# Moving three experts of each pair into the next pair, and convolving two channel pairs on TensorE with folded weights

## The chip, the cores and the metric

The kernel runs on one core of one Trainium2 chip, in one launch. The metric is the device time of that launch in microseconds (us). A core has TensorE (matmuls, with the loading of their weights as instructions of their own), VectorE, ScalarE, GpSimd and SyncE, which here issues most of the DMAs; they run their own instruction lists and meet through semaphores. TensorE's clock is granted at one of two levels, 1.2 or 2.4 GHz, and the profile shows which (0.50 or 1.00).

## The reference, cut to what matters

Eight sequences of 256 tokens with 128 channels pass two layers, all in float32:

```python
x = x + gated_delta(layernorm(x))        # layer 0: 8 key heads, 16 value heads of 64
x = x + moe_176(layernorm(x))            # layer 0: 8 routed experts (best 2), 1 shared, hidden 176
x = x + attention_block(layernorm(x))    # layer 1: 16 heads of 8, then a dense MLP 128-512-128
x = x + moe_512(layernorm(x))            # layer 1: 1 shared and 8 routed experts (best 2), hidden 512

# inside gated_delta
mixed = hidden @ W_qkv.T                                       # 2048 channels
y = conv(mixed over time, conv_w, 4 taps, causal, depthwise)   # one filter per channel
mixed = silu(y)                                                # then queries, keys, values

# moe_512
shared_out + sum_e gates[..., e] * (gelu(x @ up[e]) @ down[e]) + x
```

The convolution is linear and has one filter per channel, so that `y[t] = sum_k conv_w[:, k] * (W hidden[t - 3 + k])`: the tap can be multiplied into the weights first.

## The kernel before, in words

**Phase 1** (lines 727 to 815 on ScalarE, 1197 to 1294 on TensorE, 1751 to 1816 on VectorE) is the gated delta layer. It is written out for ten turns; in a turn three sequences are at work: `i` has its outputs and its state computed, `n` its decays, its key products and the inverse of its triangular blocks, `f` its projections and its convolution. Sixteen tiles of 128 channels are projected in eight pairs (`project`, L979, one PSUM bank per pair): pairs 0 and 1 are queries, 2 and 3 keys, 4 to 7 values. For each pair ScalarE copies the last tap's product out of PSUM (`seed`, L602), VectorE adds the three other taps with six multiply-adds (`convolve`, L1595) and ScalarE applies silu (`silu`, L611). TensorE multiplies keys with queries and keys (`key_products`, L1012), VectorE scales the products by the decays (L1663, L1665) and inverts the 32x32 blocks in 62 small steps (L1677, L1680), between which it does the elementwise work of sequence `i`; its last step (L1687) releases TensorE's small solves (`solve32`, L1050 and L1051), which are followed by merges (L1062 to L1076). Before them TensorE makes the output gates (`gate`, L961). The products of the queries with the state (`from_state`, L1160) are taken by VectorE at L1747.

**Phase 2** (`pair_layers` on each engine) takes two sequences, 512 tokens, at a time. Its four steps on TensorE are: the first experts' up matmuls (L1330) and down matmuls (L1348 to L1360), whose results VectorE merges in chunks of 128 tokens (L1900, semaphore `merged`) and normalises twice (`norm`, L1559 to L1572); the attention, from the transposes of the normalised tokens (L1308) over the projections (L1365), the rotated queries and keys (VectorE L1923 to L1927, TensorE L1374), scores (L1394, L1400), softmax and values to the output projection (L1489); after a layernorm the dense MLP (L1494, gelu L895, L1499); after another the router (L1314) and the nine experts (`up`, L1513, gelu on ScalarE L903, `down`, L1522, and VectorE's accumulation into `x2`, L1977). The order on TensorE is up(0), and then up(e + 1) and down(e) for each expert. Behind down(4) the tokens of the next pair are transposed (`turn_first`). Pairs 0 to 2 run in a hardware loop (`Fori`), pair 3 is written out behind it. SyncE loads the next pair once all four chunks are merged and stores a pair when its last expert has been added.

The order of all this is written by hand: each engine's list is fixed, and the semaphore counts in the waits say what must have ended.

## Time and profile before

| | us |
|---|---|
| median of 3 runs (lowest, highest) | 1685.59 (1682.43, 1690.14) |
| the profiled execution | 1669.67 |
| its span, first to last instruction | 1667.9 |
| TensorE busy in the span | 1368.3 (82%) |
| VectorE busy | 911.9 (55%) |
| ScalarE busy | 723.2 (43%) |
| GpSimd busy | 195.3 (12%) |
| mean granted TensorE clock | 0.843 |

The times are of one execution taken by the hardware profiler, from the start of the span. Phase 1 ends near 816 us with the first load of phase 2. A busy share says little by itself here: both phases are chains in which the bound moves from one engine to another. PE is TensorE's matmuls, PEld its weight loads, DVE VectorE, ACT ScalarE, POOL GpSimd, SP SyncE. A float32 matmul stands in the profile as two instructions, each with its own weight load, so that four matmuls of 512 columns are counted as x8.

### The profile page before, as it was taken

How to read it: one execution, taken by the hardware profiler on the slowest of the kernel's cores; microseconds unless marked ns; L12 is line 12 of the kernel's file. 1: busy time of each engine (PE TensorE's matmuls, PEld its weight loads, DVE VectorE, ACT ScalarE, POOL GpSimd, SP SyncE). 2: the span in 40 equal slices, each digit the busy share in tenths (PEclk: the TensorE clock that was granted, in tenths of full speed). 3: DMA queues.
4: the chain of work that ended last, by engine and by line, in shares of the span. 5: the costliest groups of instructions: out<-in, count | busy, mean ns of one | idle time of the engine just before them, and what ended most of it. 6: DMA issues, size and time to landing. Idle time of an engine off the chain costs nothing.

```text
span 1667.9 us, 27801 instructions
## 1 busy us (share of the span) xinstructions
PE 1368.3 (82%) x11040; PEld 984.9 (59%) x11048; DVE 911.9 (55%) x2365; ACT 723.2 (43%) x1347; POOL 195.3 (12%) x188
## 2 busy tenths in 40 slices
PE   2768897988879888878588789877899768997689
PEld 2456666676757667568455466653676435764356
DVE  4687979787887969681354222552224621255221
ACT  1646473746565564724232333423324233342332
POOL 5011212112121212110100000000000000000000
PEclk9768898887978787876796899968999689996899
DMA  3000000000000000003000000000000000000000
GB/s 113 4 1 4 2 11 1 1 10 2 10 2 10 2 7 2 29 1 138 12 7 1 1 1 8 1 7 1 1 8 1 7 1 1 7 1 1 1 0 7
DMA packets 15076, 17.80 MB, mean 11 GB/s; under 512 B 2567, under 2 KB 13216, under 8 KB 14560
## 3 DMA queue, kind: packets, MB, share of 16 engines
q1 hardware_dynamic: 12768, 14.09, 2.6%
q8 instruction: 91, 1.49, 0.4%
q0 software_dynamic: 576, 1.76, 0.3%
q10 hardware_dynamic: 1600, 0.12, 0.1%
q14 instruction: 41, 0.34, 0.1%
HBM read 13.87 MB, written 2.10 MB: 10 GB/s over the span
## 4 chain that ended last, share of the span: by engine, by line
PE 36%; issue 32%; DVE 23%; ACT 6%; POOL 2%; DMA 1%; SPq 0%; POOLq 0%; DVEq 0%; ACTq 0%
PE ps L1012 4%; DVE arena L1677 4%; DVE arena L1680 4%; PE ps L1513 4%; PE ps L1522 4%; PE ps L994 4%; DVE arena L1595 2%; PE ps L1494 1%; PE ps L1330 1%; PE ps L979 1%; POOL rstd L508 1%; PE ps L1138 1%; ACT arena L611 1%; PE ps L991 1%; PE ps L1125 1%
## 5 line engine op out<-in xcount | busy, mean ns | idle before, releaser
L1595 DVE SCALAR_TENSOR_TENSOR arena<-ps,conv_w,arena 128x255 f32<-128x255 f32 (+2 forms) x384 | 163.6, 475 | 19.5 <-ACT arena L602 15.0
L1522 PEld LDWEIGHTS ps<-arena 128*128 128x128 f32 x1152 | 133.7, 192 | 15.3 <-issue 14.6
L903 ACT ACTIVATE arena<-ps 128x512 f32<-128x512 f32 x144 | 86.0, 597 | 127.9 <-PE ps L1513 127.9
L1513 PE MATMUL ps<-arena 128*128 128x512 f32 x288 | 135.3, 617 | 0.0
L1522 PE MATMUL ps<-arena 128*128 128x128 f32 x1152 | 133.8, 275 | 0.0
L1977 DVE SCALAR_TENSOR_TENSOR arena<-ps,rw,arena 128x128 f32<-128x128 f32 x128 | 36.0, 343 | 139.0 <-PE ps L1522 139.0
L508 POOL TENSOR_TENSOR rstd<-var_eps,half_power 128x2 f32<-128x2 f32 (+1 forms) x28 | 23.3, 832 | 748.2 <-DVE var_eps L1566 748.2
L1012 PE MATMUL ps<-arena 64*128 64x256 f32 x256 | 84.0, 468 | 16.4 <-ACT arena L611 16.4
L1012 PEld LDWEIGHTS ps<-arena 64*128 64x128 f32 x256 | 53.4, 225 | 62.3 <-DVE arena L1665 27.2
L1663 DVE TENSOR_TENSOR arena<-ps,arena 128x512 f32<-128x512 f32 x64 | 44.1, 689 | 84.2 <-PE ps L1012 73.9
L468 POOL TENSOR_TENSOR arena<-con,log_decay 128x512 f32<-128x512 f32 x64 | 68.3, 1078 | 178.4 <-PE ps L994 78.5
L1513 PEld LDWEIGHTS ps<-arena 128*128 128x128 f32 x288 | 55.0, 200 | 57.1 <-issue 57.1
L979 PE MATMUL ps<-arena 128*128 128x256 f32 x256 | 80.7, 450 | 8.8 <-DVE arena L1595 8.0
L1680 DVE TENSOR_TENSOR arena<-arena 128x30 f32<-128x30 f32 (+14 forms) x240 | 83.1, 346 | 8.2
L1677 DVE TENSOR_TENSOR arena<-arena 128x30 f32<-128x30 f32 (+14 forms) x240 | 83.0, 346 | 7.0
L994 PE MATMUL ps<-arena,con 128*128 128x512 f32 x128 | 83.8, 743 | 0.0
L581 ACT ACTIVATE arena<-ps,log_beta 128x128 f32<-128x128 f32 x256 | 70.9, 378 | 29.0 <-PE ps L994 28.7
L1308 PE MATMUL ps<-con,h_tok 128*128 128x128 f32 x48 | 13.4, 435 | 82.0 <-DVE h_tok L1572 82.0
L979 PEld LDWEIGHTS ps<-arena 128*128 128x128 f32 x256 | 53.6, 226 | 31.1 <-DVE arena L1595 17.9
L482 POOL TENSOR_TENSOR o_rstd<-ssq,half_power 128x16 f32<-128x16 f32 x16 | 47.0, 2936 | 212.6 <-DVE ssq L1715 212.6
L602 ACT ACTIVATE arena<-ps,conv_w 128x256 f32<-128x256 f32 x128 | 51.7, 485 | 44.9 <-PE ps L979 44.6
L1935 DVE TENSOR_REDUCE arena<-ps 128x8 f32<-128x2048 f32 (+1 forms) x24 | 54.3, 2289 | 30.6 <-PE ps L1400 30.6
(247 smaller groups left out, 2988.5 us busy)
## 6 DMA issues: line engine op xcount, KB each, us to landing
arena<-in_routed_up SPq DMA_DIRECT2D x1, 2048.0 KB, 9.9
arena<-in_routed_down SPq DMA_DIRECT2D x1, 2048.0 KB, 14.5
x_ln<-in_x SPq DMA_DIRECT2D x8, 128.0 KB, 2.3
arena<-in_w_mix SPq DMA_DIRECT2D x1, 1024.0 KB, 9.7
x_in<-in_x SPq DMA_DIRECT2D x8, 128.0 KB, 2.5
...
```

The lines of the kernel that those rows point to most:

```text
L468: pool.tensor_tensor(gm[k % NB].rearrange("p (h n) -> p h n", h=BATCH), over_heads(upto, BATCH), over_last(log_decay[n % 2][:, c, BATCH * ...
L581: ins = act.activation(dm[n % 2][:, BATCH * k + h, :], ps[:, k % 2, h * P:(h + 1) * P], ACT.Exp, bias=log_beta[n % 2][:, c, v:v + 1])
L903: act.activation(hid1[e % 2][:, i, :], ps[:, i, :], ACT.Gelu).then_inc(s["mgelu"], 1)
L979: mm = pe.matmul(ps[:, PAIR_BANK[p], j * SEQ:(j + 1) * SEQ], w_mix[:, m * P:(m + 1) * P], hT3[:, f % 3, :], start=True, stop=True)
L994: pe.matmul(ps[:, k % 2, :], beyond, gm[k % NB], start=False, stop=True, skip_group_check=True)\
L1012: mm = pe.matmul(ps[:, KK_BANK[k % 2], 2 * P * g:2 * P * (g + 1)].rearrange("p (q n) -> p q n", q=2), mix_qk[n % 2][r:r + DH, QK_TILES + m ...
L1513: pe.matmul(ps[:, i, :], m_up[:, e, i * P:(i + 1) * P], hT, start=True, stop=True)\
L1522: mm = pe.matmul(ps[:, 4 + e % 2, c * P:(c + 1) * P], hid1[e % 2][:, i, c * P:(c + 1) * P], m_down[:, e, i, :], start=(i == 0), stop=(i == ...
L1595: ins = dve.scalar_tensor_tensor(conv_tile(f, m)[:, sh:SEQ], ps[:, PAIR_BANK[p], j * SEQ:(j + 1) * SEQ - sh], conv_w[:, m, TAPS - 1 - sh:T ...
L1677: me.did(dve.tensor_tensor(tmp, inv[:, j + 1:BLOCK, j:j + 1].to_broadcast([P, rows, j]), inv[:, j:j + 1, 0:j].to_broadcast([P, rows, j]), ...
L1680: me.did(dve.tensor_tensor(inv[:, j + 1:BLOCK, 0:j], inv[:, j + 1:BLOCK, 0:j], tmp, ALU.subtract))
L1935: dve.tensor_reduce(heads, sc, X_AXIS, ALU.max, negate=True).then_inc(s["max_ready"], 1)
```

## The change

Experts: the last three of the nine (6, 7 and 8) of pairs 0 to 2 are no longer computed at the end of their pair but at three places of the next pair; pair 3 keeps all nine. Their input `hT_m` (the transposed tokens) and the sum `x_m` get storage of their own, the gates too, and a pair is stored when its ninth accumulation has been made. All loops over pairs are written out. The attention's weights are loaded after phase 1 instead of in its last turns, because `eps` now lies in the storage of `xs64`.

Convolution: for channel pairs 0 and 1 four weight matrices each with one tap multiplied in (`w_tap`) are made once at the start, by sixteen scaled identities on VectorE, four matmuls with ones that spread a tap over the partitions, and four products. TensorE then makes projection and convolution of such a tile in four matmuls over shifted columns that accumulate in PSUM, and ScalarE applies silu straight from PSUM. The two pairs drop out of `seed`, `convolve` and `silu`, and pair 2 is projected where pair 0 was.

VectorE makes the folded weights once, at the start:

```diff
+            dve.memset(v_tok[:, 0, 0:2, :], 1.0).then_inc(s["tap_ones"], 1)
+            for m in range(2 * FOLDED):
+                for tap in range(TAPS):
+                    dve.tensor_scalar(w_tap[:, m, tap, :], ident, conv_w[:, m, tap:tap + 1], None, ALU.mult)\
+                        .then_inc(s["tap_diag"], 1)
+            for m in range(2 * FOLDED):
+                dve.wait_ge(s["tap_psum"], m + 1)
+                dve.tensor_tensor(w_tap[:, m, :, :], ps[:, m, :].rearrange("p (a b) -> p a b", a=TAPS),
+                                  over_heads(w_mix[:, m * P:(m + 1) * P], TAPS), ALU.mult).then_inc(s["taps_ready"], 1)
```

TensorE in phase 1:

```diff
+            def convolve_folded(f, m, n, has_n):
+                p, j = m // 2, m % 2
...
+                for sh in range(TAPS):
+                    mm = pe.matmul(ps[:, PAIR_BANK[p], j * SEQ + sh:(j + 1) * SEQ], w_tap[:, m, TAPS - 1 - sh, :],
+                                   hT3[:, f % 3, 0:SEQ - sh], start=(sh == 0), stop=(sh == TAPS - 1), skip_group_check=True)
...
-                    project(f, 0, n, has_n)
+                    project(f, 2, n, has_n)
...
-                    project(f, 1, n, has_n)
+                    convolve_folded(f, 0, n, has_n)
                 if has_i:
                     from_state(i, 0, (6, 7), (("s_ready", i + 1), ("r_ready", 2 * i + 1)), "qs_psum")
                     solve(i, 1, 0)
                 if has_f:
-                    project(f, 2, n, has_n)
+                    convolve_folded(f, 1, n, has_n)
...
                             gate(i, n, c, j, has_i)
+                if has_f:
+                    convolve_folded(f, 2, n, has_n)
+                    convolve_folded(f, 3, n, has_n)
+                if has_n:
                     solve32(i, n, 0, has_i)
```

ScalarE in phase 1 (the second call stands ahead of `solved32`; the seeds and silus of pairs 0 and 1 go):

```diff
-                    seed(f, 0)
-                    seed(f, 1)
+                    silu_folded(f, 0)
...
+                if has_f:
+                    silu_folded(f, 1)
```

SyncE in phase 2:

```diff
+            for it in range(PAIRS):
+                if it + 1 < PAIRS:
+                    sp.wait_ge(s["merged"], G * it + G)
+                    sp.dma_start(pair_in[:, :, :], pair(out, it + 1)).then_inc(s["pair_loaded"], 16)
+                if it > 0:
+                    sp.wait_ge(s["mdown_used"], EXPERTS * it)
+                    sp.dma_start(pair(out, it - 1), x_m[:, :, :]).then_inc(s["x_stored"], 16)
```

TensorE in phase 2, behind the first FFN's down matmuls, behind the output projection and behind the dense MLP's down matmuls:

```diff
+                if it > 0:
+                    pe.wait_ge(s["merged"], it * G + 2)
+                    up(it - 1, LATE[0], LATE_BANKS[0])
+                    pe.wait_ge(s["merged"], it * G + G)
+                    down(it - 1, LATE[0], LATE_DOWN[0], 0)
                 turn_tokens(1, h_tok, 4)
...
+                if it > 0:
+                    up(it - 1, LATE[1], LATE_BANKS[1])
+                    down(it - 1, LATE[1], LATE_DOWN[1], 1)
                 turn_tokens(2, h_tok, 5)
...
+                if it > 0:
+                    up(it - 1, LATE[2], UP_BANKS)
+                    down(it - 1, LATE[2], LATE_DOWN[2], 1)
+                turn_tokens(3, h_tok, 6)
+                route(hT_m, m_rt[:, :])
+                up(it, 0, UP_BANKS)
+                here = LATE[0] if more else EXPERTS
+                for e in range(here):
+                    if e + 1 < here:
+                        up(it, e + 1, UP_BANKS)
+                    down(it, e, 4 + e % 2, e % 2)
                     if more and e == AHEAD:
                         turn_first(it + 1)
```

ScalarE in phase 2, the first late expert's gelus between two table switches (the others stand ahead of `transpose_out(2)` and `transpose_out(3)`):

```diff
+                if it > 0:
+                    load_table(ACT.Gelu)
+                    hidden(it - 1, LATE[0], LATE_BANKS[0], 0)
                 load_table(ACT.Exp)
```

VectorE in phase 2, ahead of the rotation (the two others stand behind `norm(5)` and `norm(6)`), and the loops of all engines:

```diff
+                if it > 0:
+                    accumulate(it - 1, LATE[0], LATE_DOWN[0])
...
-            with pe.Fori(0, PAIRS - 1) as it:
-                pair_layers(it, True)
-            pair_layers(PAIRS - 1, False)
+            for it in range(PAIRS):
+                pair_layers(it, it + 1 < PAIRS)
```

`LATE` is (6, 7, 8), `LATE_BANKS` ((0, 1, 0, 1), (1, 2, 3, 5)), `LATE_DOWN` (6, 6, 5). `up` waits for the gelus of the expert before only where the banks are still in use; `down` waits for its gelus and for the accumulation two experts back.

## Rows read from the trace of the kernel before

**Rows 1.** Stretches: from:to, length, busy us (PE, PEld, DVE, ACT, POOL), clock, DMA share, GB/s

```profile
1080.30:1089.60 9.30, 0.00 (x0) 0.00 (x0) 7.45 (x34) 0.00 (x0) 1.39 (x2) 0.67 0.10 29
1152.00:1158.50 6.50, 0.00 (x0) 0.00 (x0) 5.23 (x15) 0.27 (x2) 3.50 (x3) 0.74 0.00 0
...
1186.00:1241.00 55.00, 55.00 (x323) 40.54 (x322) 9.79 (x39) 20.44 (x34) 1.02 (x1) 1.00 0.00 1
```

**Rows 2.** Chain that ended last, router and first experts of pair 2: start us, us, what

```profile
1389.24 1.87 PE ps L1314 x8
1391.11 8.51 PE ps L1513 x16
1399.62 3.57 PE ps L1522 x32
1403.19 3.44 PE ps L1513 x8
```

**Rows 3.** The same chain, the dense MLP's first matmuls of pairs 1, 2 and 3

```profile
1160.53 6.12 PE ps L1494 x8
...
1372.16 6.11 PE ps L1494 x8
...
1580.53 6.04 PE ps L1494 x8
```

**Rows 4.** TensorE in order of time, pair 1: start, us, what, [idle before <- releaser]

```profile
1089.65 1.12 PE L1308 MATMUL ps<-con,h_tok 128*128 128x128 f32 x4 [9.36 <-DVE h_tok L1572]
1091.64 5.49 PE L1365 MATMUL ps<-arena 128*128 128x384 f32 x8 [0.87 <-ACT arena L830]
...
1101.37 0.81 PE L1394 MATMUL ps<-causal_bf,ident_bf 128*128 128x512 bf16 x3
```

**Rows 5.** TensorE in order of time, end of the attention to the router, pair 1

```profile
1150.82 1.16 PE L1489 MATMUL ps<-arena 128*128 128x128 f32 x8 [0.69 <-ACT arena L890]
1158.54 1.11 PE L1308 MATMUL ps<-con,h_tok 128*128 128x128 f32 x4 [6.56 <-DVE h_tok L1572]
...
1175.81 1.12 PE L1308 MATMUL ps<-con,h_tok 128*128 128x128 f32 x4 [4.57 <-DVE h_tok L1572]
```

**Rows 6.** VectorE in order of time, second merge's layernorm and last rotation, pair 1

```profile
1084.79 0.49 DVE L1559 BATCH_NORM_STATS2 stats<-arena 128x6 f32<-128x128 f32 x2
...
1098.64 0.42 DVE L1927 TENSOR_TENSOR arena<-arena 128x256 f32<-128x256 f32 x1
```

**Rows 7.** ScalarE in order of time, ahead of the key products, one sequence

```profile
485.62 0.84 ACT L602 ACTIVATE arena<-ps,conv_w 128x256 f32<-128x256 f32 x2 [2.51 <-PE ps L979]
...
494.92 0.63 ACT L611 ACTIVATE arena<-arena 128x512 f32<-128x512 f32 x1
```

**Rows 8.** TensorE's waits in one turn of the pair loop: us in total, times, longest

```profile
PE ps L1314 <- issue: 2.1, 1, 2.1
```

**Rows 9.** VectorE in order of time, the last two convolutions of that sequence

```profile
490.60 5.28 DVE L1595 SCALAR_TENSOR_TENSOR arena<-ps,conv_w,arena 128x255 f32<-128x255 f32 x12 [1.42 <-ACT arena L602]
```

**Rows 10.** TensorE in order of time, projection and query-times-state products, next sequence

```profile
537.37 1.03 PE L979 MATMUL ps<-arena 128*128 128x256 f32 x4
538.33 1.16 PE L1160 MATMUL ps<-arena 64*128 64x128 f32 x16
```

**Rows 11.** TensorE, the first of the small solves in two sequences

```profile
378.92 0.21 PE L1050 MATMUL ps<-arena 32*32 32x32 f32 x1 [1.43 <-DVE arena L1687]
...
562.70 0.26 PE L1050 MATMUL ps<-arena 32*32 32x32 f32 x1 [4.75 <-DVE arena L1687]
```

**Rows 12.** A stretch of the sequence of the 1.43 us row (columns as in rows 1)

```profile
353.00:366.00 13.00, 13.00 (x55) 12.29 (x54) 11.61 (x25) 4.35 (x10) 2.98 (x1) 0.50 0.01 1
```

**Rows 13.** VectorE, GpSimd and TensorE at the start, each in order of time

```profile
21.07 0.60 DVE L1572 TENSOR_SCALAR h_tok<-x_ln,mv,rstd 128x128 f32<-128x128 f32 x2 [2.40 <-POOL rstd L454]
...
17.49 2.85 POOL L447 TENSOR_SCALAR arena<-arena,norm_w 128x1024 f32<-128x1024 f32 x1 [3.00 <-DMA arena<-in_w_out]
...
20.48 1.94 PE L923 MATMUL ps<-con 128*128 128x128 f32 x8 [20.48 <-POOL arena L447]
```

254 lines of the change are left out of this document (141 added, 113 removed).

## The prediction

> **What bounds the kernel now.** I read the stretches table first, then each stretch's own chain of waits, then each engine in order of time around the places that the diff touches. Phase 1 (the gated delta layer, eight sequences in one unrolled pipeline) ends near 816 us and phase 2 (four pairs) takes the rest. The pairs repeat: the first 512-column matmuls of the dense MLP start at 1160.53, 1372.16 and 1580.53 us [rows 3], so a pair takes 211.63 us inside the loop and 208.37 us where pair 3, written out behind the loop, follows pair 2.
>
> Inside a pair the reader is to see two kinds of stretch. The expert stretch is pure TensorE: busy 55.00 of 55.00 us at full clock, VectorE 9.79, ScalarE 20.44 [rows 1]. Its chain is a strict alternation of 3.44 us (four up matmuls) and 3.57 us (four chunks of down) [rows 2], 7.01 us per expert. The other kind is TensorE standing still for a layernorm: 9.36 us ahead of the attention [rows 4], 6.56 and 4.57 us ahead of the dense MLP and the router [rows 5], at a granted clock of 0.67 and 0.74 of 2.4 GHz on the mean of the first two [rows 1]. What follows them runs at the lower level, 1.2 GHz: eight 512-column instructions took 6.12 us [rows 3], where the same shape takes 3.44 us in the expert stretch [rows 2].
>
> Phase 1 is a ring of all engines. Per sequence (about 92.6 us) the ends that matter are: ScalarE's last silu ahead of the key products [rows 7]; VectorE, without a pause, from the products through the 32x32 inverse; and TensorE's small solves, which start when VectorE's inverse is turned [rows 11].
>
> **Phase 2, experts moved.** Experts 6, 7 and 8 of pairs 0 to 2 leave the expert stretch: 3 pairs x 3 x 7.01 = 63.1 us off the path. They come back, each as eight up and 32 down instructions, at three places of the next pair.
>
> (a) Behind the first FFN's down matmuls, ahead of the attention's transposes. The place is 9.36 us long [rows 4]. Up costs 3.44 us plus about 0.3 us for two waits on the gelus (only two banks), then the wait for the fourth merged chunk, which VectorE ends some 4.5 us into the gap (the second layernorm pair begins at 1084.79 [rows 6]), then down, 3.57: it ends about 1.2 us before the transposes can start. Cost 0. The cover is the two layernorms; without them it would be 7.9 us. What is queued behind that wait on TensorE is only the down itself. ScalarE pays two more table switches and four gelus while it has no other work. VectorE's four accumulations (1.13 us, the price of the other experts' groups) stand ahead of the rotation, where it waits for the projections anyway. Since TensorE no longer rests, I expect the transposes (1.12) and the projections (5.49 us, 1.37 a chunk [rows 4]) at half these times. The first chunk is then ready 0.5 + 0.7 = 1.2 us earlier, and VectorE's rotation, whose last operation ends at 1098.64 + 0.42 = 1099.06 now [rows 6], ends at 1097.9. TensorE, which now begins the query and key transposes only behind all projections and needs some 4.2 us for them, has one of four chunks left by then, 1.05 us. So the scores start 9.3 us behind the first transposes and not 11.7 (1089.65 to 1101.37 [rows 4]): 2.4 us gained.
>
> (b) Behind the output projection: 1150.82 + 1.16 = 1151.98 to 1158.54 is free [rows 5]. Up 3.44, last gelu 0.7, down 3.57: it ends at 1159.8, 1.3 us late. (c) Behind the dense MLP's down: 3.44 + 0.7 + 3.57 = 7.7 us in a gap of 4.57, so 3.1 us late. Against that, everything from 1158.5 on meets a warm array: the eight MLP instructions 3.44 instead of 6.12, two sets of transposes 0.65 instead of 1.12, the route about 1.1 instead of 1.87 and the first two ups 6.88 instead of 8.51 [rows 2, 3, 5]. From the end of the output projection to the end of the second up it takes 36.0 us now and 3.44 + 0.7 + 3.57 + 1.6 + 3.44 + 0.8 + 3.6 + 3.44 + 0.7 + 3.57 + 1.4 + 1.1 + 6.88 = 34.2 us then: 1.8 us gained with two experts inside.
>
> So pairs 1 to 3 gain 2.4 + 1.8 = 4.2 us each, 12.6 us. The store of a pair now waits for its ninth accumulation in the next pair, and VectorE's first accumulation there waits for that store: it has over 10 us (route, two ups, one down) for one transfer, cost 0; on SyncE the load of the next pair stands ahead of it and needs nothing of it. The attention weights are now fetched behind the first pair's load instead of before phase 2's start; they are wanted 60 us later, cost 0 to 1 us.
>
> (d) The loops over pairs are written out. At the loop's turn TensorE waits 2.1 us, once per turn, for nothing but issue [rows 8] and the clock falls; the turn without a loop is the 3.26 us shorter one. Two turns: 6.5 us. Phase 2 together: 63.1 + 12.6 + 6.5 = 82.2 us less.
>
> **Phase 1, two pairs of channels on TensorE.** Removed per sequence: 12 of VectorE's 48 multiply-adds (5.28 us for twelve [rows 9]), four ScalarE copies, two silus over SBUF, four 256-column matmuls. Added: sixteen 256-column matmuls and two silus from PSUM. The 5.3 us of VectorE buy nothing by themselves: the last two convolutions wait for ScalarE's copies, 1.42 us in the row [rows 9], and these wait for TensorE's projections; both stay where they are. What counts is ScalarE's queue, which is full from 485.6 until the last silu ends at 495.55 [rows 7]; two silus of about 0.55 us leave it: 1.1 us, seven times, 7.7 us gained. The last convolution then ends last, and caps it there.
>
> Costs. One matmul of 256 columns is 0.5 us (1.03 for two, tail included [rows 10]) at full clock and 0.86 at half. First, four matmuls stand in place of two ahead of the query-times-state products; those end at 538.33 + 1.16 = 539.49 [rows 10], just when VectorE asks for them (it had no pause there): no slack where the clock is low; I estimate 1 us where it is full, from the two groups ahead at half their time. So 0.9 us in two of six sequences, 1.8. Second, the last eight matmuls (3.5 us) go into TensorE's rest ahead of the small solves, 4.75 us in one sequence, 1.43 us in another, which follows 13 us at half clock [rows 11, 12]. With the 0.9 us pushed in front, cost 0 in four sequences and 1.5 and 5 in two: 6.5 us. If the cover were gone it would be 4.4 us each. Third, a busier TensorE keeps the clock a little longer into the solves; I take 0.5 us x 7 = 3.5 us gained. The bounds are 0 and the 4.7 us that the half-clock work there could give back.
>
> The Trainium skill speaks against the folding: its page "TensorE: Matmul & The Clock Gate", section "Part 3: Packing small matmuls", has weight loads overlap running matmuls only where row groups differ, and gives 128 / 1.2 ns for one. By that rule the 24 added instructions would each show 0.107 us, 2.6 us a sequence, and the sum would come out 21 us longer. The trace does not agree: 32 full-height down instructions of 128 columns, each with its own load, take 3.57 us, 0.112 each [rows 2], with no room for a load.
>
> **The start.** VectorE now makes sixteen scaled identities (128x128) and four folded weights (128x512, behind one matmul each) before the first layernorm, whose result was there at 21.67 us [rows 13]. The trace has no such scaling; the nearest are 0.30 us for one 128x128 normalisation, two in 0.60 [rows 13], so about 4.8 us from 17.7 on, and beside GpSimd's 2.85 us [rows 13] perhaps later. TensorE is held until 20.48 and has 1.94 us of transposes [rows 13]; then four 512-column matmuls (3.44 us at full clock [rows 2], twice that at half), and VectorE's last product 0.7: 29.3 us. The layernorm itself, with GpSimd's root in it, takes about 2.4 (the row before shows 2.40 of waiting for GpSimd, most of it for the 2.85 us operation). Its result comes at about 31.7, 10 us late; six convolutions instead of eight then make up 5.3 us. Cost 5 us, bounds 0 and 10.
>
> Phase 1 together: -7.7 + 1.8 + 6.5 - 3.5 + 5 = +2 us.
>
> **The sum.** 1669.7 us (the profiled execution; its span is 1667.9) - 82 + 2 = 1589.7, a ratio of 0.952. The median of the runs shown is 1685.59, 1% above the profiled one; the same ratio gives 1605 us.
>
> **The rivals.** (1) Phase 1 spills: TensorE's rest ahead of the solves is too short in most sequences. 5 us more in each of seven, 35 us: 1640 us. For it: the 1.43 us row [rows 11]; against: 4.75 us. (2) Weight loads show: each of the 24 instructions added per sequence waits for its own load, 40.54 / 322 = 0.126 us [rows 1], 3.0 us a sequence, 24 us in eight: 1629 us. Against it: the 0.112 us per down instruction [rows 2]. (3) The clock is kept through the dips of phase 1: what took half clock ahead of the key products and behind them halves, some 5 us in each of seven: 1570 us. (4) The gaps grant only half clock to the moved experts: 14.0 us each in places of 9.4, 6.5 and 4.6 us is 21.6 us late against 21.0 saved; phase 2 keeps only the loop's gain: 1680 us, no change. Against: the clock was 1.00 before each gap and the moved work leaves no rest. (5) Slower: all twelve additional matmuls of a sequence lie on the path at half clock, 12 x 0.86 = 10.3 us, eight times, plus 10 at the start, 92 us against 82: 1697 us. It decides once TensorE has no rest left ahead of the solves and of the state products, which needs half clock through the 92.6 us of a sequence; 4.75 us of rest [rows 11] says no.
>
> **Chances.** Forecast 0.68, (1) 0.12, (2) 0.03, (3) 0.11, (4) 0.03, (5) 0.03. The range reaches 27 us down, most of the way to (3), and to (1) above: 1578 to 1640. About 0.5% is what a measurement of this kernel can tell from no change; so faster 0.94, same 0.03, slower 0.03.
>
> **What would show it.** Starts of the dense MLP's matmuls 187 to 189 us apart from pair to pair, at 3.4 us for eight; six alternations in pairs 0 to 2 and nine in pair 3; waits of TensorE for the layernorm at the three places 1.3 us or none; a late expert in each at 3.44 and 3.57; the scores 9.3 us behind the transposes. In phase 1: the first layernorm's result near 31.7 us, ScalarE's queue 1.1 us shorter, small solves starting on VectorE's turn in most sequences. Wrong it would be if the clock's mean falls in phase 2, if VectorE or ScalarE ends last in the late experts, or if phase 1's length moves by more than 15 us.

## The result, and the profile after

The changed kernel takes 1604.11 us (median; 1602.58 to 1605.23) against 1684.01 us (1676.69 to 1690.14) of the kernel before, a ratio of 0.954 with a 95% interval of 0.952 to 0.957. The forecast was 1605 us. Run once more among the experiments, it came to 0.959 (0.956 to 0.962). The profiled execution took 1602.58 us with a span of 1600.7.

The traces of the two profiled executions differ by less than that: 1667.9 - 1600.7 = 67.2 us of span, where the medians differ by 79.9. The execution of before that was profiled was near the short end of its runs. Where the 67.2 us lie is read from the starts of the dense MLP. The chain that ended last in the changed kernel shows them (start us, us, what), with the late expert ahead of the one in pair 1:

```profile
958.90 5.71 PE ps L1582 x8
...
1137.34 3.45 PE ps L1425 x8
1141.46 3.84 PE ps L1434 x32
...
1146.61 3.71 PE ps L1582 x8
...
1330.98 3.71 PE ps L1582 x8
...
1515.31 3.71 PE ps L1582 x8
```

The pairs are 187.7, 184.4 and 184.3 us apart, where they were 211.6, 211.6 and 208.4 [rows 3 has the last three starts; the first was 948.9]. From the first of these starts to the last it is 556.4 us and was 631.6, 75.2 less; from the last to the end 85.4 and was 87.4. That is 77.2 us gained in phase 2. But the first start came at 958.9 and not at 948.9: ten microseconds lost ahead of it.

The expert stretch behind the first two ups is what it was [rows 2], 3.44 and 3.57 in turn, six times and not nine. What changed is what was the gaps [rows 1, 4, 5]. The stretches table (from:to, length, busy us of PE, PEld, DVE, ACT, POOL, clock, DMA share, GB/s):

```profile
1072.00:1090.00 18.00, 14.43 (x128) 10.56 (x128) 10.98 (x33) 6.33 (x14) 1.37 (x2) 0.98 0.06 16
...
1146.00:1161.00 15.00, 12.93 (x65) 8.40 (x66) 3.69 (x17) 5.69 (x9) 2.29 (x2) 1.00 0.00 0
```

The granted clock is 0.98 and 1.00 where the gaps of before had 0.67 and 0.74 [rows 1]. TensorE in order of time at the first place of pair 1 (start, us, what, [idle before <- releaser]):

```profile
1066.26 3.70 PE L1425 MATMUL ps<-arena 128*128 128x512 f32 x8
1070.94 3.84 PE L1434 MATMUL ps<-arena 128*128 128x128 f32 x32 [0.98 <-DVE arena L2003]
1075.78 0.66 PE L1362 MATMUL ps<-con,h_tok 128*128 128x128 f32 x4 [1.00 <-DVE h_tok L1655]
1077.37 2.85 PE L1447 MATMUL ps<-arena 128*128 128x384 f32 x8 [0.93 <-ACT arena L852]
...
1085.04 1.03 PE L1479 MATMUL ps<-causal_bf,ident_bf 128*128 128x512 bf16 x4
```

The late expert ends at 1074.78; the transposes still wait 1.00 us for VectorE's layernorm, where they waited 9.36 [rows 4]. They and the projections take half their time, and the first score instructions stand 9.26 us behind the transposes (11.72 before). The other two places:

```profile
1136.18 1.16 PE L1574 MATMUL ps<-arena 128*128 128x128 f32 x8 [0.69 <-ACT arena L923]
...
1145.14 0.60 PE L1362 MATMUL ps<-con,h_tok 128*128 128x128 f32 x4
1146.61 3.70 PE L1582 MATMUL ps<-arena 128*128 128x512 f32 x8 [0.87 <-ACT arena L852]
1151.09 3.84 PE L1587 MATMUL ps<-arena 128*128 128x128 f32 x32 [0.78 <-ACT arena L930]
...
1162.72 0.60 PE L1362 MATMUL ps<-con,h_tok 128*128 128x128 f32 x4
1164.01 1.06 PE L1368 MATMUL ps<-m_rt,arena 128*128 128x8 f32 x8 [0.69 <-ACT arena L850]
1164.92 7.11 PE L1425 MATMUL ps<-arena 128*128 128x512 f32 x16
```

No wait for a layernorm is left there: both late experts overrun their gaps. From the end of the output projection (1137.34) to the end of the second up (1172.04) it takes 34.70 us with two experts inside. Neither the store of a pair nor the later fetch of the attention's weights shows a wait: the only DMA wait of phase 2 on the compute engines is 4.8 us for the first pair's load, and it was 4.7 before.

Phase 1 has two places to look at. VectorE in order of time, where it multiplies the query-times-state products, then where it turns the inverse:

```profile
446.08 1.29 DVE L1830 TENSOR_TENSOR arena<-ps,ends 128x512 f32<-128x512 f32 x2 [0.99 <-PE ps L1210]
...
652.39 2.23 DVE L1770 STREAM_TRANSPOSE arena<-arena 128x1024 f32<-128x1024 f32 x1
```

and TensorE ahead of the small solves in two sequences:

```profile
377.70 2.09 PE L1028 MATMUL ps<-arena 128*128 128x253 f32 x9
380.37 0.21 PE L1100 MATMUL ps<-arena 32*32 32x32 f32 x1 [0.57 <-DVE arena L1770]
...
652.76 2.95 PE L1028 MATMUL ps<-arena 128*128 128x255 f32 x13
655.64 0.21 PE L1100 MATMUL ps<-arena 32*32 32x32 f32 x1
```

In the upper two rows the folded matmuls (L1028) end in time and TensorE waits for VectorE's turned inverse. In the lower two they run on until 655.7, past the end of the turning (654.62), and the solves start 3.25 us behind the start of the turning, not 2.23: the kind of spill that was forecast, here 1.0 us.

### The profile page after: what moved, and what is told of

Its sections match the earlier page's. It is cut to its first block, busy times and chain, and to the rows that moved or that the text cites. A ratio compares the mean times of both kernels' runs of the same rounds, so it can differ in the third digit from the quotient of the medians.

```text
span 1600.7 us, 27174 instructions
## 1 busy us (share of the span) xinstructions
PE 1389.8 (87%) x11248; PEld 1007.2 (63%) x11248; DVE 878.9 (55%) x2290; ACT 717.6 (45%) x1321; POOL 193.0 (12%) x186
## 4 chain that ended last, share of the span: by engine, by line
PE 65%; DVE 21%; ACT 8%; issue 3%; POOL 1%; DMA 1%; SPq 0%; ACTq 0%; DVEq 0%; POOLq 0%
PE ps L1434 7%; PE ps L1425 7%; PE ps L1384 6%; PE ps L1062 5%; PE ps L1044 4%; DVE arena L1760 3%; DVE arena L1763 3%; ACT arena L914 2%; PE ps L1485 2%; PE ps L1188 2%; DVE arena L2003 2%; PE ps L1517 2%; PE ps L1028 2%; PE ps L1120 2%; PE ps L1015 2%
## 5 line engine op out<-in xcount | busy, mean ns | idle before, releaser
L866 ACT ACTIVATE arena<-ps 128x512 f32<-128x512 f32 x144 | 85.3, 597 | 163.6 <-PE ps L1425 163.5
L1678 DVE SCALAR_TENSOR_TENSOR arena<-ps,conv_w,arena 128x253 f32<-128x253 f32 (+2 forms) x288 | 123.3, 475 | 53.3 <-ACT arena L613 49.9
L1434 PEld LDWEIGHTS ps<-arena 128*128 128x128 f32 x1152 | 133.2, 192 | 25.5 <-issue 11.0
L1924 DVE SCALAR_TENSOR_TENSOR arena<-ps,gates,arena 128x128 f32<-128x128 f32 x128 | 36.0, 344 | 131.4 <-PE ps L1434 131.4
L1425 PEld LDWEIGHTS ps<-arena 128*128 128x128 f32 x288 | 52.9, 194 | 56.2 <-issue 51.9
L592 ACT ACTIVATE arena<-ps,log_beta 128x128 f32<-128x128 f32 x256 | 70.9, 378 | 26.1 <-PE ps L1044 25.8
L914 ACT ACTIVATE arena<-ps 128x512 f32<-128x512 f32 x96 | 49.6, 602 | 46.1 <-PE ps L1517 46.1
L1188 PE MATMUL ps<-arena 128*128 128x64 f32 x512 | 69.8, 301 | 0.0
L1188 PEld LDWEIGHTS ps<-arena 128*128 128x128 f32 x512 | 69.3, 218 | 0.3
L1986 DVE SCALAR_TENSOR_TENSOR arena<-ps,b,arena 128x512 f32<-128x512 f32 x56 | 41.4, 749 | 48.6 <-ACT arena L877 48.3
## 6 DMA issues: line engine op xcount, KB each, us to landing
arena<-in_routed_down SPq DMA_DIRECT2D x1, 2048.0 KB, 12.9
arena<-in_w_mix SPq DMA_DIRECT2D x1, 1024.0 KB, 10.9
```

What stands on the lines that cost most here:

```text
L592: ins = act.activation(dm[n % 2][:, BATCH * k + h, :], ps[:, k % 2, h * P:(h + 1) * P], ACT.Exp, bias=log_beta[n % 2][:, c, v:v + 1])
L866: act.activation(hid1[half][:, i, :], ps[:, banks[i], :], ACT.Gelu).then_inc(s["mgelu"], 1)
L914: act.activation(probsT[u % 2][:, j, :], ps[:, 4 + j, :], ACT.Exp).then_inc(s["probs_ready"], 1)
L1188: mm = pe.matmul(ps[:, (7, 5)[g], h * DH:(h + 1) * DH], dm[i % 2][:, VH * c + v, :], eps[:, v, :], start=True, stop=True)
L1425: pe.matmul(ps[:, banks[i], :], m_up[:, e, i * P:(i + 1) * P], hT_m, start=True, stop=True)\
L1434: mm = pe.matmul(ps[:, bank, c * P:(c + 1) * P], hid1[half][:, i, c * P:(c + 1) * P], m_down[:, e, i, :], start=(i == 0), stop=(i == HT1 - 1))
```

## The experiments

Two ways of reading are used: the ratio to before, whose interval is about 0.004 wide on either side (6 us), and the parts of the profiled execution. This table is worked out from the order-of-time views of each; all times in us. "Inverse" is the start of the last turned inverse of phase 1, "stretch" goes from there to the first dense MLP, "pairs" are the distances of the dense MLPs, "tail" is the rest of the span, and "solves" is the length of the last sequence's second-chunk solves.

| kernel | ratio (95%) | inverse | stretch | pairs | tail | solves |
|---|---|---|---|---|---|---|
| before | 1 | 744.8 | 204.1 | 211.6 211.6 208.4 | 87.4 | 3.79 |
| whole change | 0.954 (0.952-0.957) | 744.7 | 214.2 | 187.7 184.4 184.3 | 85.4 | 6.53 |
| e1 late only | 0.953 (0.949-0.957) | 742.6 | 206.6 | 189.2 183.8 184.4 | 85.4 | 3.78 |
| e2 fold only | 1.001 (0.998-1.004) | 749.5 | 210.0 | 211.6 211.7 208.4 | 87.3 | 6.54 |
| e3 loops only | 0.995 (0.993-0.998) | 747.9 | 214.1 | 205.7 210.3 208.0 | 87.3 | 6.28 |
| e4 first place only | 0.983 (0.978-0.987) | 745.4 | 207.0 | 198.6 201.0 198.1 | 87.2 | 3.78 |
| e5 second, third place | 0.967 (0.963-0.970) | 743.6 | 206.3 | 198.7 194.6 194.6 | 85.3 | 3.78 |
| e6 filled gaps | 0.982 (0.978-0.986) | 746.2 | 207.5 | 207.3 201.3 201.4 | 84.0 | 3.79 |
| e7 query first | 0.955 (0.951-0.958) | 748.2 | 214.3 | 187.7 184.4 184.3 | 85.4 | 6.54 |
| e8 warm pair 0 | 0.947 (0.944-0.951) | 749.0 | 202.8 | 180.1 186.2 184.4 | 85.3 | 3.78 |
| e9 whole again | 0.959 (0.956-0.962) | 750.6 | 213.8 | 189.2 183.8 184.4 | 85.4 | 6.34 |
| e10 shifted | 0.954 (0.950-0.958) | 752.4 | 213.5 | 189.2 183.8 184.4 | 85.3 | 6.44 |
| e11 warm, fold | 0.947 (0.944-0.950) | 744.0 | 199.5 | 182.4 187.6 184.4 | 85.3 | 3.78 |
| e12 warm, no fold | 0.949 (0.946-0.952) | 742.3 | 209.5 | 180.1 186.2 184.4 | 85.3 | 6.76 |

**One part alone.** e1 has the changed phase 2 with phase 1 of before, here against the changed kernel:

```diff
-FOLDED = 2
-NC = NP - FOLDED
...
                 if has_f:
-                    convolve_folded(f, 0, n, has_n)
+                    project(f, 1, n, has_n)
```

> The kernel before with phase 2 alone changed: three late experts per pair, loops over pairs written out, phase 1 as before (all eight channel pairs convolved by VectorE). Theory, phase 2 carries the whole gain: the sum gave -82 us for phase 2 and +2 for phase 1, so this kernel should be 75 to 84 us faster than the kernel before, a ratio of 0.951 to 0.955, and no slower than the whole change. First dense MLP instructions of the pairs 184 to 188 us apart. Rival, the folding carries part: then it is 5 us or more slower than the whole change (1609 us and above). What is asked besides: in the changed kernel the stretch from the last inverse of phase 1 to the first dense MLP was 10 us longer, 5.7 of it small matmuls of the last sequence at half clock. If the folding does that, it is gone here, and this kernel is some 5 us faster than the whole change (about 1599 us).

Measured: 1600.43 us, ratio 0.9528. The whole gain is here, and nothing is missing without the folding. In the profiled execution, the fastest of its six, the stretch is 206.6 us and the last sequence's solves take 3.78 us; so most of the ten microseconds, 7.6, are not lost there. Whether for want of folding, the next runs say.

e2 is the other half, against the kernel before; phase 2 keeps its loops and nine experts in each pair:

```diff
+FOLDED = 2
+NC = NP - FOLDED
...
                 if has_f:
-                    project(f, 1, n, has_n)
+                    convolve_folded(f, 0, n, has_n)
```

> The kernel before with phase 1 alone changed: two channel pairs on TensorE with folded weights; phase 2 with its loops as before (the attention weights are fetched behind the first pair's load, since the small-solve buffers now cover their place). Theory: the terms of phase 1 as predicted sum to +2 us (-7.7 ScalarE's silus, +1.8 state products, +6.5 spill, -3.5 clock, +5 start), so within 5 us of the kernel before. The trace of the whole change says the same terms came out as -9.8 (1.4 us in each of seven sequences from the turned inverse to the key products), +6.3 (0.9 us in each of seven up to the turned inverse), +1.6 (start), and +5.7 in the last sequence's solves: about +4. Rival (the folding is worth its place): 8 us or more faster. Rival (TensorE has no rest left): 20 us or more slower.

Measured: 1681.21 us, ratio 1.0008 (0.998 to 1.004): nothing, as the sum said. The rivals of 8 us faster and 20 us slower are out.

**The loops.** e3 writes them out in the kernel before and does nothing else:

```diff
-            with pe.Fori(0, PAIRS - 1) as it:
+            for it in range(PAIRS - 1):
                 pair_layers(it, True)
```

> The kernel before with the loops over pairs written out on all engines, nothing else. Theory: the turn of a loop costs TensorE 2.1 us of issue and what the clock loses by it, 3.26 us per turn, two turns: 6.5 us faster (ratio 0.996), dense MLP starts of all pairs 208.4 us apart. Rival: the last pair was shorter because it loads no next pair and turns no first tokens, and not for the loop; then nothing changes, or 2.1 x 2 = 4.2 us if only the issue goes and the clock does not.

Measured: 1671.6 us, ratio 0.9953, 7.8 us faster (interval 3 to 12). From the router's transposes of one pair to the attention's of the next it takes 122.9 and 122.7 us where the kernel before takes 125.5 twice: 2.7 us a turn, not 3.26, so 5.4 us are shown by place; the rest of the 7.8 is within the interval. Inside this span two things happen. From the end of the second up to the attention's transposes it takes 109.3 us in both turns, 4.0 less than before (113.3), which is what the turn itself costs; but the first two ups (L1513) take 10.1 and 9.9 us where they took 8.66, and give 1.2 to 1.5 of it back.

```profile
980.46 10.12 PE L1513 MATMUL ps<-arena 128*128 128x512 f32 x16
```

The run shows a second thing. Its instructions are those of before up to the first turn, and yet the stretch is 214.1 us. TensorE in order of time, solves (L1125) and outputs (L1138) of the last sequence:

```profile
791.04 6.28 PE L1125 MATMUL ps<-arena 128*128 128x64 f32 x32
797.11 7.04 PE L1138 MATMUL ps<-arena 128*128 128x64 f32 x32
```

So the ten microseconds lost in the changed kernel's trace need neither the folding nor the late experts.

**The places one by one.** e4 keeps the first place only, e5 the other two:

```diff
-LATE = (EXPERTS - 3, EXPERTS - 2, EXPERTS - 1)
+LATE = (EXPERTS - 1,)
-                    up(it - 1, LATE[1], LATE_BANKS[1])
-                    down(it - 1, LATE[1], LATE_DOWN[1], 1)
...
-                    up(it - 1, LATE[2], UP_BANKS)
-                    down(it - 1, LATE[2], LATE_DOWN[2], 1)
```

> The whole change with one late expert per pair in place of three: the one ahead of the attention; the two behind the output projection and behind the dense MLP's down matmuls stay in the expert stretch of their own pair. Theory: the first place saves 7.0 us for the expert and 2.4 for the clock per pair, the other two together 14.0 + 1.8. So this kernel is 3 x 15.8 = 47 us slower than the whole change (1651 us, ratio to before 0.980). Dense MLP starts 200 us apart. Rival, the clock has no part in it: 42 us slower than the whole change. Rival, the second and third expert overran their gaps and brought little (1.3 and 3.1 us late): 30 us or less.

Measured: 1650.6 us, ratio 0.9825, 47 us slower than the whole change by the two ratios (40 by that of e9). By the pairs and the tail it is 41.2 + 1.8 = 43.0 us, 14.3 per pair where 15.8 was forecast. The overrun rival (30 us) is out; between 42 and 47 the totals do not decide. The parts of the trace do: the six experts are 42.0 us of the difference, and from the end of the output projection to the end of the second up it takes 37.3, 35.9 and 35.8 us with no expert inside against 34.7 with two, 4.9 us more in all. So at these two places the clock does have a part, 1.6 us a pair where 1.8 was forecast. What hides it is elsewhere: in e4 the attention from its first score through its output projection is 3.4 us shorter and pair 0 by 1.1, and the fronts of the attention are 0.6 longer.

```diff
-LATE = (EXPERTS - 3, EXPERTS - 2, EXPERTS - 1)
+LATE = (EXPERTS - 2, EXPERTS - 1)
-                    up(it - 1, LATE[0], LATE_BANKS[0])
-                    pe.wait_ge(s["merged"], it * G + G)
-                    down(it - 1, LATE[0], LATE_DOWN[0], 0)
```

> The whole change with two late experts per pair: those behind the output projection and behind the dense MLP's down matmuls; the gap ahead of the attention stays empty. Theory: the first place is worth 7.0 us for its expert and 2.4 us for the clock of the transposes and projections behind it, per pair, so this kernel is 3 x 9.4 = 28 us slower than the whole change, ratio to before about 0.961; the scores start 11.7 us behind the first transposes again, as in the kernel before, and 9.3 in the changed one. Rival, the expert alone: 21 us slower than the whole change, and the scores at 9.3.

Measured: 1625.84 us, ratio 0.9667, so 21 us slower than the whole change, the rival's number. The trace says otherwise:

```profile
1072.48 1.12 PE L1359 MATMUL ps<-con,h_tok 128*128 128x128 f32 x4 [9.36 <-DVE h_tok L1643]
1074.53 4.24 PE L1438 MATMUL ps<-arena 128*128 128x384 f32 x8 [0.93 <-ACT arena L852]
...
1082.95 1.03 PE L1467 MATMUL ps<-causal_bf,ident_bf 128*128 128x512 bf16 x4
```

The gap of 9.36 us is back, the transposes take 1.12 again, and the scores start 10.5 us behind them (10.9 in pair 2). The pairs are 11.0, 10.2 and 10.3 us longer than in the whole change, 31.5 in all: 21.0 for the three experts, 4.5 for the three fronts of the attention (1.5 each, forecast 2.4), 7.3 for a longer attention behind them, less 1.3 in pair 0. Of these 31.5, 7.9 are hidden in the span, because this execution has the short stretch (206.3 against 214.2); whether its five other executions have it too was not profiled. A total that mixes the two is no measure of a place; the parts are.

**The clock alone.** e6 moves no expert. It fills the gaps of pairs 1 to 3 with matmuls whose result nobody reads (loops written out):

```diff
+                if it > 0:
+                    pe.wait_ge(s["merged"], it * G + 2)
+                    for _ in range(10):
+                        pe.matmul(ps[:, 1, :], ident, w1[:, 0:4 * P], start=True, stop=True)
                 turn_tokens(1, h_tok, 4)
...
+                    for _ in range(7):
+                        pe.matmul(ps[:, 1, :], ident, w1[:, 0:4 * P], start=True, stop=True)
                 turn_tokens(2, h_tok, 5)
...
+                    for _ in range(5):
+                        pe.matmul(ps[:, 0, :], ident, w1[:, 0:4 * P], start=True, stop=True)
                 turn_tokens(3, h_tok, 6)
```

> The kernel before with the loops over pairs written out and no expert moved, but matmuls of 512 columns whose result nobody reads in the three gaps of pairs 1 to 3: ten ahead of the attention's transposes, seven behind the output projection, five behind the dense MLP's down matmuls (8.6, 6.0 and 4.3 us in gaps of 9.4, 6.6 and 4.6). It measures the clock's share alone. Theory: per pair 2.4 us in the attention's front, and behind the output projection 6.0 us (eight dense instructions 3.44 in place of 6.12, two sets of transposes 0.9 less, the route 0.8 less, the first two ups 1.6 less): 8.4 x 3 = 25 us faster than the kernel with the loops written out, so about 32 us faster than before, ratio 0.981. Rival, the half clock there has another cause than the empty gaps: no faster than the kernel with the loops written out, ratio 0.995. What the moved experts alone are worth is then the rest: 82 - 32 = 50 us.

Measured: 1652.94 us, ratio 0.9823: about 22 us faster than with the loops alone, for work that is useless. The rival is out: an empty gap does cost the clock behind it. TensorE in pair 1, dense MLP (L1501), transposes, router, first two ups (L1523):

```profile
1161.02 3.70 PE L1501 MATMUL ps<-arena 128*128 128x512 f32 x8 [0.87 <-ACT arena L830]
...
1173.96 0.66 PE L1308 MATMUL ps<-con,h_tok 128*128 128x128 f32 x4 [0.34 <-DVE h_tok L1582]
1175.30 1.11 PE L1314 MATMUL ps<-m_rt,arena 128*128 128x8 f32 x8 [0.69 <-ACT arena L828]
1176.27 8.75 PE L1523 MATMUL ps<-arena 128*128 128x512 f32 x16
```

The MLP, the transposes and the router are at full clock [rows 2, 3 and 5 have them at half]. The first ups are not: 8.75 us, as before. By the pairs and the tail (624.0 + 87.3 to 610.0 + 84.0) the clock's share is 17.3 us, 5.8 per pair where 8.4 was forecast; what the two spans differ by beyond that (25.6 us in all) lies ahead of the first dense MLP, where the two kernels are the same. By place the 17.3 are 6.5 at the fronts of the attention (2.2 a pair, forecast 2.4), 11.9 from the output projection to the second up (4.0 a pair, forecast 6.0, of which 1.6 is these ups), and 1.1 lost between the first score and the output projection.

**A wait removed that brings nothing.** e7 puts the folded matmuls behind the query-times-state products:

```diff
-                if has_f:
-                    convolve_folded(f, 0, n, has_n)
                 if has_i:
                     from_state(i, 0, (6, 7), (("s_ready", i + 1), ("r_ready", 2 * i + 1)), "qs_psum")
+                if has_f:
+                    convolve_folded(f, 0, n, has_n)
+                if has_i:
                     solve(i, 1, 0)
```

> The whole change with one step reordered in phase 1: the first four folded matmuls of 256 columns stand behind the query-times-state products and not ahead of them. In the changed kernel VectorE waits 0.99 us for these products in the sequence that starts the inverse at 430 us, and the time from the inverse's first transposition to the last is 0.9 us above the kernel before in six of seven sequences. Theory: that wait is the 0.9 us; it goes, the inverse takes 36.0 us again in place of 36.9, and the kernel is 0.9 x 6 = 5.4 us faster than the whole change (1679 x 0.9544 - 5.4 = 1597 us). Rival, the small solves of the second chunk, now behind the folded matmuls, become late by as much: no change.

Measured: 1606.59 us, ratio 0.9545 against 0.9544 of the whole change: no change, the rival's result. VectorE in order of time at the same operation as above, and TensorE ahead of the small solves of the same sequence as above:

```profile
449.35 1.29 DVE L1831 TENSOR_TENSOR arena<-ps,ends 128x512 f32<-128x512 f32 x2
...
654.98 2.22 DVE L1771 STREAM_TRANSPOSE arena<-arena 128x1024 f32<-128x1024 f32 x1
```

```profile
654.82 3.60 PE L1028 MATMUL ps<-arena 128*128 128x256 f32 x16
658.35 0.21 PE L1100 MATMUL ps<-arena 32*32 32x32 f32 x1
```

The wait of 0.99 us is gone and the inverse takes 36.0 us instead of 36.9 in each of these sequences. But the folded matmuls now spill in six sequences, by 1.1 us, where three had it in the change's first profile and five in e9's and e10's, and from the turned inverse to the key products it takes 27.1 us on the mean of the last six where e9 and e10, in the order of the change, take 26.1 to 26.2. The 0.9 us move from VectorE's half of the ring (the cycle in which each engine waits for the other once a sequence) to TensorE's. The place of the rival was wrong (the small solves of the second chunk were named; it is those of the first level and what follows them), its sum was right.

**The rests that are left.** e8 fills the rests in which no expert can stand: ahead of the last sequence's small solves, ahead of phase 2, and in pair 0.

```diff
+                elif has_n:
+                    for _ in range(5):
+                        pe.matmul(ps[:, PAIR_BANK[1], :], ident, w1[:, 0:4 * P], start=True, stop=True)
...
+            for _ in range(5):
+                pe.matmul(ps[:, 0, :], ident, w1[:, 0:4 * P], start=True, stop=True)
             turn_first(0)
...
+                if it == 0:
+                    for _ in range(6):
+                        pe.matmul(ps[:, 1, :], ident, w1[:, 0:4 * P], start=True, stop=True)
                 if it > 0:
                     up(it - 1, LATE[1], LATE_BANKS[1])
```

> The whole change with matmuls of 512 columns whose result nobody reads, in the rests that no late expert fills: five ahead of the last sequence's small solves (a rest of 5.3 us), five ahead of phase 2's first transposes (9.75 us), and nine, six and four in pair 0 at the places where the later pairs have their late experts. Theory, the rests cost the clock and the clock costs time behind them: up to 3 us in the last small solves, 5.1 from the first transposes to the end of the first FFN (49.3 us in pair 0, 44.1 in pair 1), 3.3 in the attention (64.8 against 61.5 from its transposes to the end of the projection), 6.0 behind it, so 14 to 18 us faster than the whole change (about 1587 us), and further 6 us where the last sequence's solves then stay at full clock. The first dense MLP then starts some 12 us earlier than at 958.9. Rival, the clock in pair 0 falls for other reasons: within 3 us of the whole change. Rival, at half clock the added matmuls overrun their rests (0.86 us becomes 1.7 each): slower by up to 5 us.

Measured: 1593.39 us, ratio 0.9471 (0.944 to 0.951), 12 us below the whole change (19 by e9's ratio), less than the 14 to 18 of the theory and beyond the rivals. By its parts: the stretch is 202.8 us (214.2), the first pair 180.1 (187.7), the second 186.2 (184.4), and phase 1, whose instructions are the same until its last sequence, ends 4.3 us later: 11.4 + 7.6 - 1.9 - 4.3 = 12.8 us; the spans have 12.9 (1600.7 to 1587.8). Not all of the 11.4 is the fills' doing: 6.0 of it is that the last sequence's solves and outputs are at full clock here, and e12 below, with the same five fills ahead of that sequence's small solves, has them at half (6.76 us). Beside e4 and e5, the kernels with folding, without fills and with the solves at full clock, the stretch is 4.2 and 3.5 us shorter.

e11 fills more: nine ahead of phase 2, three ahead of the last head transposes.

```diff
-            for _ in range(5):
+            for _ in range(9):
                 pe.matmul(ps[:, 0, :], ident, w1[:, 0:4 * P], start=True, stop=True)
             turn_first(0)
...
+                if has_i and not has_n:
+                    for _ in range(3):
+                        pe.matmul(ps[:, 0, :], ident, w1[:, 0:4 * P], start=True, stop=True)
```

> The whole change with more matmuls that nobody reads: as in the kernel with pair 0 warmed (five ahead of the last sequence's small solves, nine, six and four in pair 0), but nine in place of five ahead of phase 2's first transposes, where 4.08 us of rest were left and the route and the first ups behind it still ran at half clock, and three ahead of the last sequence's head transposes, where TensorE rests 4.6 us. Theory: transposes 0.65 for 1.12, route 1.1 for 1.85, ups some 3 us shorter: 4 us faster than the kernel with pair 0 warmed, 0.945 of before. Rival: the nine run at half clock, 10.3 us, and hold the transposes back by 1 to 3 us: no gain over it.

Measured: 1589.56 us, ratio 0.9473 (0.944 to 0.950), no gain over e8. TensorE from the last fills (L1627) to the router (L1375) and the first ups of pair 0; in e8 these three rows read 1.11, 1.85 and 2.06 us:

```profile
808.78 7.89 PE L1627 MATMUL ps<-arena,con 128*128 128x512 f32 x18
818.57 0.66 PE L1361 MATMUL ps<-con,h_tok 128*128 128x128 f32 x4 [1.90 <-DVE h_tok L1674]
820.01 1.03 PE L1375 MATMUL ps<-gate_w,arena 128*128 128x8 f32 x8 [0.78 <-ACT arena L842]
820.89 1.10 PE L1391 MATMUL ps<-arena 128*128 128x512 f32 x2
```

So the mechanism is as expected, the fills did not overrun, and the stretch is 3.3 us shorter. The first two pairs are 2.2 and 1.3 us longer. In this execution the gain is there and is given back; the total is the rival's, but not for the rival's reason.

e12 is e11's filling on e1, without the folding:

```diff
-                if has_f:
-                    convolve_folded(f, 0, n, has_n)
+                if has_f:
+                    project(f, 1, n, has_n)
```

> The same added matmuls, with phase 1 as in the kernel before: no folding. Theory: folding is worth nothing either way (with phase 1 alone changed the ratio was 1.0008, with phase 2 alone changed 0.9528 against 0.9544 for the whole), so this kernel is within 5 us of the same kernel with folding. Rival: with the clock held up in the last sequence and in phase 2 the folded matmuls bring 0.5 us or more per sequence to light: 5 us or more slower than with folding.

Measured: 1591.91 us, ratio 0.9492, 3 us above e11, inside both intervals. The folding is worth nothing that these runs can tell. Both e8 and e11 are faster than the kernel before and the changed one.

**The same kernel twice.** e9 is the changed kernel without any edit.

> The whole change, once more, unchanged. In the traces so far the stretch from the last turned inverse of phase 1 to the first dense MLP took 204 to 207 us in three kernels and 210 to 214 us in four others, and kernels whose instructions are the same up to there stand in both groups. Theory: it is how the falls of the clock come to lie in that execution, not the change; so this run's stretch may be 204 as well as 214 us, and the ratio to before is 0.954 within 0.004. Rival: the stretch belongs to the kernel; then it is 214 us again and the time within 2 us of 1604.

Measured: 1609.04 us, ratio 0.9586 (0.956 to 0.962), just outside the 0.950 to 0.958 expected; stretch 213.8 us. Its phase 1 ends 5.9 us later than in the first profile of the same instructions, and its first pair is 1.5 us longer. The long stretch is what the rival said, the time is not (1604 within 2 us); this run alone does not choose between them.

e10 delays the start by two fills on VectorE:

```diff
+            for k in range(2):
+                dve.memset(v_tok[:, 0, :, :], 1.0).then_inc(s["tap_ones"], 1)
+                dve.wait_ge(s["tap_ones"], k + 1)
             dve.memset(v_tok[:, 0, 0:2, :], 1.0).then_inc(s["tap_ones"], 1)
```

> The whole change with two fills of 1024 elements per partition on VectorE ahead of the folded weights, some 2.2 us of delay at the start of the kernel and nothing else. Theory, the same as for the run before: later work meets the falls of the clock at other places, so parts of phase 1 and the stretch to the first dense MLP change by several us in either direction while their instructions are the same, and the whole is anywhere from 5 us faster to 8 us slower than the whole change. Rival, the kernel is simply shifted: 0 to 2.2 us slower, each stretch as long as before within 0.5 us.

Measured: 1603.39 us, ratio 0.9536, faster than e9, of which it is the delayed form. Its executions are 1608.8, 1610.5 and 1610.6 us on the one hand, with a mean clock of 0.861 to 0.863, and 1594.2, 1595.4 and 1597.9 on the other, with 0.870 to 0.874. One kernel, and two groups some 14 us apart; the first three executions are the slower one. The first group fits e10's own rival, a kernel simply shifted by 0 to 2.2 us, if it is laid beside e9 (1609.04 us); the second fits it beside neither run of the changed kernel. Only the first group was profiled, with the long stretch (213.5 us), so that the short stretch is in the other is a guess.

Where the two forms of the stretch part is seen between e4 and the whole change. Up to pair 0 they have the same instructions. The solves (L1171 and L1175) and outputs (L1184 and L1188) of the last sequence, e4 first:

```profile
788.86 3.79 PE L1171 MATMUL ps<-arena 128*128 128x64 f32 x32
792.48 3.74 PE L1184 MATMUL ps<-arena 128*128 128x64 f32 x32
```

```profile
788.23 6.53 PE L1175 MATMUL ps<-arena 128*128 128x64 f32 x32
794.55 7.04 PE L1188 MATMUL ps<-arena 128*128 128x64 f32 x32
```

and the stretches table of 774 to 828 us and of four microseconds in it, e4 and then the whole change:

```profile
774.00:828.00 54.00, 34.44 (x249) 30.50 (x248) 19.30 (x50) 9.49 (x14) 10.74 (x9) 0.75 0.31 115
...
788.00:792.00 4.00, 3.93 (x42) 3.73 (x40) 3.34 (x6) 0.60 (x1) 0.51 (x1) 1.00 0.74 311
```

```profile
774.00:828.00 54.00, 36.91 (x236) 34.29 (x234) 17.48 (x35) 7.27 (x11) 10.74 (x9) 0.66 0.31 115
...
788.00:792.00 4.00, 3.93 (x25) 3.77 (x21) 2.75 (x5) 0.53 (x1) 1.13 (x1) 0.61 0.63 266
```

From 780 to 788 us both are at full clock (1.00). In the whole change it falls at the start of these 64 instructions (0.61 from 788 to 792, then 0.50), in e4 behind them (1.00 until 802, then 0.69), and that is 2.7 + 3.3 us at once. Of the fourteen profiles above, the seven with solves at 3.8 us have stretches of 199 to 208 us, and the seven with solves over 6 us have 209 to 214. The Trainium skill, page "TensorE: Matmul & The Clock Gate", section "Part 1: The HAM clock gate (the "warmup" mystery)", says that the gate's rhythm is not restarted by a kernel, so the same kernel meets the change of clock at different instructions from run to run. The traces agree with it as far as they go: the same instructions end phase 1 at 744.7 us in the first profile and at 750.6 in e9, and e10 comes in two groups. That this rhythm is the cause of either is not shown.

## Why the prediction was right, point by point

**The total was right, by more luck than its working shows.** The ratio was forecast as 0.952 and is 0.954 (0.959 in e9). The forecast of the profiled execution was 1589.7 us and that execution took 1602.58; the 13 us between are the ten lost ahead of the first dense MLP and five missing in phase 2, less the two that phase 1 was to cost and in this profile did not. The median hides them, since the profiled execution of before was 14 us under its own median and that of after 1.5 under its own. Scaling the sum by a ratio came out right because such shifts are as large as the misses.

**Phase 2: forecast 82.2 us, found 77.2.** The nine experts (63.1 us) go as forecast: six alternations at 3.44 and 3.57 remain. Front of the attention: forecast 2.4 us a pair, found 11.72 - 9.26 = 2.5 in pair 1, 7.7 in the three. Output projection to the second up: forecast 34.2 us against 36.0, found 34.70; 1.3 and not 1.8 gained (3.9 in the three), since the waits on the gelus and the down matmuls' ends came to a little more. Loops: forecast 6.5. The turn itself costs 4.0 us, as e3 shows, so 8.0 in two; in e3 the first ups of the pairs give 1.2 to 1.5 us a turn back, in the changed kernel only pair 0 does (ups of 10.1 us for 8.66, 1.2 us from its dense MLP to their end), since the others run at full clock; that leaves 6.8. If nothing else had moved, these would make 63.1 + 7.7 + 3.9 + 6.8 = 81.5 us, close to the 82.2. The step that failed is the one that is not in the sum: that the attention between its first score and its output projection stays as it is. The stretches table, before and then after:

```profile
1101.30:1152.00 50.70, 43.57 (x475) 26.38 (x474) 17.96 (x18) 17.72 (x33) 0.00 (x0) 0.80 0.01 1
```

```profile
1085.00:1137.40 52.40, 46.14 (x479) 27.69 (x478) 18.09 (x19) 17.72 (x32) 0.00 (x0) 0.77 0.00 1
```

Same instructions, a mean clock of 0.77 in place of 0.80, and 1.7 us more; 1.6 and 1.1 more in pairs 2 and 3, 4.3 in all. That gives 81.5 - 4.3 = 77.2, what was measured. Why this part is slower is not shown. That the clock kept by a filled gap is lost at the next thin stretch is a tempting reason, but the other kernels do not bear it out: in pairs 1 to 3 this part takes 48.2, 53.5 and 51.0 us in e3, with empty gaps, 50.8, 52.0 and 50.4 in e4, with the gap ahead of it filled, and 56.3, 53.8 and 53.7 in e5, with that gap empty. The three together take 152 to 164 us in the kernels of the table, a spread larger than the 4.3. The sign that the prediction named for phase 2, starts 187 to 189 us apart, does not follow from its own sum, which gives 208.4 - 21.0 - 4.2 = 183.1; found were 187.7, 184.4 and 184.3.

**Each place.** Forecast 9.4 us per pair for the first and 15.8 for the other two. Against e3, the first alone brings 8.8 a pair (e4), the other two alone 12.7 (e5); on top of the others, 10.5 and 14.3. Together it is 23.2 a pair where 25.2 was forecast. The differences of whole pairs hold the attention's variation too. By place, the clock's share beside the experts was forecast as 4.2 a pair and is 2.6 + 1.3 = 3.9 in the changed kernel; with fills it was forecast as 8.4 and is 2.2 + 4.0 = 6.2 in e6, 5.8 net. So the clock terms have the right sign and place, and only those of the fills were sized too large, by a quarter to a third.

**The ten microseconds ahead of the first dense MLP** had no term at all. Six of them are a fall of the clock at another instruction (the 2.7 + 3.3 us above), and the same is in e3, which has nothing of the change there. The rest is in pair 0, whose instructions up to there are those of before: 1.7 us from its first transposes to the attention's and 3.5 in the attention from its first score on, less 1.0 at the attention's front. The prediction took what one profile shows as what the kernel does; its range had no width for that, and it was wide enough for other reasons.

**Phase 1: forecast +2 us, found 0 within 5.** e2 gives +1.3 us (-4 to +6). Over the profiles, the five kernels without folding turn their last inverse at 742.3 to 747.9 (744.8 on the mean), the nine with it at 743.6 to 752.4 (746.9 without the delayed e10): the two microseconds of the forecast may be there, but the spread is larger. The terms: the state products cost 0.9 to 1.1 us in six sequences and not in two; the step that failed is the 1 us of slack that was estimated for a full clock: there is none, as VectorE asks for them within 0.1 us in every sequence of before. The spill is 1.0 us, in three sequences in the first profile and five in e2, e9 and e10; 3 to 5 us where 6.5 was forecast, in more sequences and smaller. ScalarE's queue: two silus less, and the last silu ends 9.04 us behind the first row and not 9.93 [rows 7], 0.9 for 1.1; with the clock kept by the folded matmuls it is 1.6 us a sequence from the turned inverse to the key products including the spill (27.8 to 26.2 in e9 and e10), where the terms had 0.7. The start:

```profile
18.95 4.19 DVE L1632 TENSOR_SCALAR arena<-con,conv_w 128x128 f32<-128x128 f32 x16
24.77 0.69 DVE L1636 TENSOR_TENSOR arena<-ps,arena 128x512 f32<-128x512 f32 x1 [1.62 <-PE ps L961]
...
29.82 0.60 DVE L1655 TENSOR_SCALAR h_tok<-x_ln,mv,rstd 128x128 f32<-128x128 f32 x2 [0.91 <-POOL rstd L466]
```

The sixteen identities take 4.19 us (forecast 4.8), the first layernorm's result is there at 30.42 (forecast 31.7). The first inverse then starts 3 us later than without folding on the mean of the kernels (82.1 against 79.1; forecast 5). And e7 adds what the sum of terms could not: each sequence is a ring in which 0.9 us taken from one half come back in the other, so the terms do not add.

**The rivals.** (1) Spill of 5 us a sequence: the place is right, the size is 1.0 us, in three to five sequences. (2) Visible weight loads: TensorE's last gate matmuls and the folded ones behind them, in one sequence:

```profile
461.57 3.70 PE L1000 MATMUL ps<-arena 128*128 128x512 f32 x8
465.11 3.60 PE L1028 MATMUL ps<-arena 128*128 128x256 f32 x16
```

As many columns, twice the loads, and no more time: no load shows. By the rule of the Trainium skill's page "TensorE: Matmul & The Clock Gate", section "Part 3: Packing small matmuls", and the load time of 128 / 1.2 ns that the same page gives in its section "LDWEIGHTS (loading the stationary operand)", the sum would by estimate have been 21 us longer; the trace does not agree with it here either. (3) The clock kept through phase 1 (1570 us): in e9 and e10 1.6 us a sequence are gained from the turned inverse on, with the spill of 1.0 paid and ScalarE's 0.9 in it. If these simply add, the clock's part is some 1.7 us, an estimate, more than the 0.5 of the sum and less than the rival's 5. (4) Half clock for the moved experts: the clock is 0.98 to 1.00 there. (5) All added matmuls on the path: no.
